# Attention on one core: the softmax sums' reciprocals are copied out of PSUM by ScalarE, earlier in a slot, and VectorE multiplies the context straight out of its PSUM bank, one step earlier

## The reference

```python
h = layernorm(x, gamma1, beta1)
Q = (h @ Wq + bq).reshape(B, T, 16, 32).transpose(0, 2, 1, 3)      # K and V alike
scores = jnp.einsum('bhqd,bhkd->bhqk', Q, K) / np.sqrt(32)
scores = jnp.where(causal, scores, -jnp.inf)
attn = jax.nn.softmax(scores, axis=-1)
ctx = jnp.einsum('bhqk,bhkd->bhqd', attn, V)
ctx = ctx.transpose(0, 2, 1, 3).reshape(B, T, C)
x1 = x + ctx @ Wo + bo
...
x2 = x1 + gelu(layernorm(x1) @ W1 + b1) @ W2 + b2
x = x + gate * (x2 - x)
```

## Time and profile before

| | |
|---|---|
| three runs | 1737.58, 1741.61, 1746.10 us; median 1741.61 |
| the profiled execution | 1743.59 us, of which the span from first to last instruction is 1741.6 |
| PE busy | 1660.3 us, 95% of the span |
| DVE, ACT, POOL busy | 1174.9, 976.4, 439.6 us |
| mean granted TensorE clock | 0.982 of full speed |

### The profile page before, as it was taken

One profiled execution on the slowest core, in us unless ns is written; L12 is line 12 of the kernel. 1 busy time (PEld: TensorE's weight loads), 2 busy tenths in 40 slices (PEclk: granted clock), 3 DMA queues, 4 the chain that ended last, 5 costly groups with the idle time before them and its releaser, 6 DMA issues.

```text
span 1741.6 us, 27454 instructions
## 1 busy us (share of the span) xinstructions
PE 1660.3 (95%) x9416; PEld 1335.6 (77%) x9416; DVE 1174.9 (67%) x2759; ACT 976.4 (56%) x2257; POOL 439.6 (25%) x670
## 2 busy tenths in 40 slices
PE   5899998899999999999999889999999999999999
PEld 3678766667676777776777558888999999999998
DVE  6899875776776768686866736767565656565643
ACT  5788853777676767676767654635242424242422
POOL 6788620323131322323232112010101010101010
PEclk9999998899999999999999989999999999999999
DMA  7122234343444435343433534576646464646451
GB/s 285 73 87 84 82 118 115 96 99 88 117 101 102 116 84 130 87 122 88 103 86 86 179 113 158 207 267 250 252 160 254 167 245 166 245 170 242 170 194 67
DMA packets 61826, 254.81 MB, mean 146 GB/s; under 512 B 10580, under 2 KB 15956, under 8 KB 45944
## 3 DMA queue, kind: packets, MB, share of 16 engines
q1 hardware_dynamic: 61688, 253.06, 44.6%
HBM read 153.93 MB, written 48.23 MB: 116 GB/s over the span
## 4 chain that ended last, share of the span: by engine, by line
PE 79%; DVE 9%; ACT 4%; DMA 3%; issue 2%; SPq 2%; POOL 1%; DVEq 0%; POOLq 0%; ACTq 0%
PE psum L82 21%; PE psum L84 20%; PE psum L83 20%; PE psum L1634 4%; PE psum L1662 4%; PE psum L1615 3%; PE psum L1540 2%; DVE psum L1167 1%; SPq L922 1%; ACT psum L1410 1%; PE psum L1558 1%; ACT k_exps L1420 1%; DVE k_tokens L1218 1%; DMA k_stack<-k_samples 1%; PE psum L1566 1%
## 5 line engine op out<-in xcount | busy, mean ns | idle before, releaser
L1410 ACT ACTIVATE psum<-psum,b_mx 128x512 f32<-128x512 f32 (+3 forms) x512 | 258.4, 506 | 200.7 <-DVE b_mx L1167 198.8
L1167 DVE CUSTOM_DVE_ANT_0 psum<-psum,b_mask 128x512 f32<-128x512 f32 (+3 forms) x512 | 244.7, 505 | 151.4 <-PE psum L1615 149.6
L2477 ACT ACTIVATE k_act<-k_stack_f,k_smalls 128x512 f32<-128x512 f32 x112 | 81.0, 723 | 337.3 <-DVE k_stack_f L2265 337.3
L1420 ACT ACTIVATE k_exps<-psum 128x512 f32<-128x512 f32 (+1 forms) x384 | 203.0, 530 | 21.9 <-PE psum L1634 19.9
L2118 POOL TENSOR_SCALAR k_result<-k_result,k_pb 128x512 f32<-128x512 f32 x32 | 59.9, 1887 | 449.1 <-DVE k_result L2184 449.1
L1634 PE MATMUL psum<-k_stack 98*128 98x512 f32 (+3 forms) x512 | 157.8, 350 | 13.3 <-ACT k_exps L1420 13.2
L2244 DVE TENSOR_TENSOR k_act_lo<-k_act,k_act_hi 128x512 fp32r<-128x512 f32 x112 | 77.4, 691 | 130.4 <-ACT k_act_hi L2480 130.4
L1615 PE MATMUL psum<-k_stack 96*128 96x512 f32 (+3 forms) x512 | 150.5, 336 | 2.3 <-ACT psum L1410 2.3
L82 PE MATMUL psum<-k_act_hi,k_w_hi 128*128 128x512 f32 x384 | 151.0, 393 | 0.6 <-DVE k_act_lo L2244 0.6
L83 PE MATMUL psum<-k_act_lo,k_w_hi 128*128 128x512 f32 x384 | 150.6, 392 | 0.0
L84 PE MATMUL psum<-k_act_hi,k_w_lo 128*128 128x512 f32 x384 | 150.3, 391 | 0.0
(11 more groups left out here) (368 smaller groups left out, 4568.0 us busy)
## 6 DMA issues: line engine op xcount, KB each, us to landing
k_stack<-w_factors SPq DMA_DIRECT2D x35, 1792.0 KB, 7.8
k_stack<-k_samples SPq DMA_DIRECT2D x384, 128.0 KB, 2.4
k_weights<-w_factors SPq DMA_DIRECT2D x17, 1792.0 KB, 7.7
x<-k_tokens SPq DMA_DIRECT2D x10, 1024.0 KB, 3.9
k_tokens<-x SPq DMA_DIRECT2D x8, 1024.0 KB, 4.9
d<-k_result SPq DMA_DIRECT2D x32, 256.0 KB, 2.5
k_raw<-x SPq DMA_DIRECT2D x8, 1024.0 KB, 4.9
k_raw<-d SPq DMA_DIRECT2D x8, 1024.0 KB, 7.0
```

The source lines that it names most:

```text
L1167: last = dve.tensor_tensor_reduce(got, got, mask[:, S - width:S], -INV_SQRT_DH, -2.0 * MASKED, ALU.add, ALU.min, mx[n % 2][:, h, t:t + 1])
L1410: act.activation(sc(n, u)[:, at:at + width], sc(n, u)[:, at:at + width], ACT.Exp, bias=mx[n % 2][:, h, t:t + 1], scale=-1.0, accum_out=sum ...
L1420: act.activation(exps[n % 2][:, h, at:at + width], by_key(n, u)[:, 0:width], ACT.Exp, scale=INV_SQRT_DH).then_inc(k_act, 1)
L2477: act.activation(act_f[:], whole_tile, ACT.Gelu, bias=small(smalls, "b1", 2 * pair % M + second)).then_inc(pair_gelu, 1)
```

## The change

Four things change together:

1. ACT no longer copies the context. It copies the turned reciprocals out of their bank (`recs_out`, into the same SBUF tile), one step after PE turned them, and that frees the bank (`pj_act` instead of `pj_dve`).
2. PE turns the reciprocals in step 3 of slots with g = 0, 1 or 2, and in step 6 of those with g = 3 (`recs_step`); before it was step 7 in all. `bank_uses` lists `bc` earlier to match.
3. DVE multiplies bank 1 by the copied reciprocals, and this multiplication now counts up `ctx_out`, for which `maxima(n, 0)` on PE waits.
4. DVE does this in step 7, after `max_unit(n, 7)`; before, it multiplied in step 8, after `maxima_out(n, 0)`.

```diff
+def recs_step(n):
+    return 6 if n % G == 3 else 3
 def bank_uses(n):
-    bc = [("bc", *divmod(n - 2, G), "dve")] if 0 <= n - 2 < GROUPS else []
+    bc = [("bc", *divmod(n - 2, G), "act")] if 0 <= n - 2 < GROUPS else []
...
     if g == 0:
-        return qk + each("st", b + 1, range(J), "dve") + bc + v + after_back
+        return qk + bc + each("st", b + 1, range(J), "dve") + v + after_back
     if g == 1:
-        return qk + each("tin", b + 1, range(T), "act") + bc + v
+        return qk + bc + each("tin", b + 1, range(T), "act") + v
     if g == 2:
-        return qk + each("tb", b + 1, range(J), "act") + bc + each("wo", b - 1, range(J - 1), "dve")
+        return qk + bc + each("tb", b + 1, range(J), "act") + each("wo", b - 1, range(J - 1), "dve")
...
         def ctx_high(n):
-            wait_taken(pool, ("bc", *divmod(n, G)))
+            pool.wait_ge(ctx_out, n + 1)
...
         def over_sums(n):
-            name = ("bc", *divmod(n, G))
-            wait_full(dve, name)
-            dve.wait_ge(ctx_out, n + 1)
-            dve.tensor_tensor(ctx_at(n), ctx_at(n), pj(name), ALU.mult).then_inc(pj_dve, 1)
+            wait_taken(dve, ("bc", *divmod(n, G)))
+            wait_context(dve, n, CTX_ORDER[-1])
+            dve.tensor_tensor(ctx_at(n), ctx_bank, ctx_at(n), ALU.mult).then_inc(ctx_out, 1)
...
-            if u == 8 and 0 <= n - 2 < GROUPS:
+            if u == 7 and 0 <= n - 2 < GROUPS:
                 over_sums(n - 2)
...
-        def context_out(n):
-            wait_context(act, n, CTX_ORDER[-1])
+        def recs_out(n):
+
+            name = ("bc", *divmod(n, G))
+            wait_full(act, name)
             if n >= G + 1:
+                act.wait_ge(cl_set, n - G)
                 wait_full(act, ("wo", (n - G - 1) // G, J - 1))
-            act.activation(ctx_at(n), ctx_bank, ACT.Copy).then_inc(ctx_out, 1)
+            act.activation(ctx_at(n), pj(name), ACT.Copy).then_inc(pj_act, 1)
...
-            if u == 7 and 0 <= n - 2 < GROUPS:
-                context_out(n - 2)
+            if u == recs_step(n) + 1 and 0 <= n - 2 < GROUPS:
+                recs_out(n - 2)
...
-            if u == 7 and 0 <= n - 2 < GROUPS:
+            if u == recs_step(n) and 0 <= n - 2 < GROUPS:
                 recs_back(n - 2)
```

## The result

| | before | after |
|---|---|---|
| median, lowest and highest of 7 executions | 1743.01 us (1737.38 to 1748.95) | 1760.28 us (1752.02 to 1763.11) |
| the profiled execution, its span | 1743.59, 1741.6 us | 1762.73, 1760.7 us |
| mean granted clock in it | 0.982 | 0.977 |

The ratio is 1.0078, with a 95% interval of 1.0058 to 1.0099: slower by 10 to 17 us. The kernel is slower, as forecast, and its median lies in the range of 1752 to 1782 but 9 us under the 1769.5. By the ratio the change costs 13.6 us, half of the 27.9 that I summed up; the two medians are 17.3 apart, the upper end of that interval. So the sign was right and the sum was not.

The account below looks back on a forecast made before the run. PE was taken to bound the kernel, busy 95% of the span. Waits of 14.3 us plus clock drops of 13.6 made 27.9 us on the median of 1741.61, forecasting 1769.5 us, with an 8-in-10 range of 1752 to 1782.

Parts of the forecast that it names:

- The release behind DVE's queue: Maxima transpose on PE waits for DVE's multiplication: 1.20 us later with g = 0, 0.83 with g = 3; 14.3 us in all.
- Nothing gives these back: PE has work queued behind the maxima transpose without another repeating wait, so the 14.3 us of added waits stay.
- the first term: The added PE waits at the transpose of the maxima, 14.3 us over all slots.
- PE's idle time of 1.8: With g = 0 PE was to stand idle 1.8 us before the maxima transpose, from about 655.86 on.
- The clock: Longer PE waits bring drops to half clock, 1.7 us each; 8 of 15 possible were taken, 13.6 us.
- The rest costs nothing: ACT's moved copy, the reciprocals' bank in step 3, later statistics and maxima going out were to add no time.
- Waits alone: Rival: the waits at the maxima transpose grow by 14.3 us but the clock stays, giving 1756; chance 0.22.
- The wait goes away: Rival: without ACT's hop the maxima transpose never waits, winning 14.3 us, giving 1727; chance 0.05.
- The bank of q is late: Rival: PE's step 3 claim stalls in perhaps five slots, 3 us more, with all 15 drops 1784; chance 0.04.
- no change: Rival: shorter waits behind the maxima transpose take back the added ones; 1745 if three quarters were absorbed; chance 0.07.

Follow-up runs that it names:

- experiment 2: Against the changed kernel, DVE's multiplication moved from step 7 to step 6 for g = 0, 1 and 2: 1751.67 us, ratio 1.0023 to the kernel before.
- experiment 3: Against the changed kernel, DVE's multiplication moved a step later, to step 8, in all slots: 1800.26 us, ratio 1.0308 to the kernel before.
- Experiment 4: Against the changed kernel, step 8's score matmul issued 13 times instead of once in 7 slots with g = 0: 1749.72 us, ratio 1.0021 to the kernel before.
- experiment 1: The changed kernel run again with no edit: 1759.21 us, ratio 1.0070 to the kernel before.
- experiment 5: Against the changed kernel, PE's transposes of the reciprocals and ACT's copy put back in step 7 in all slots: 1767.48 us, ratio 1.0108 to the kernel before.

## Why the prediction was right and wrong

- **The release behind DVE's queue: right, in place and size.** For g = 0 L1656 was to start 1.20 us later in its slot; it starts 16.21 us into the slot for 14.97, 1.24 later. For g = 3 it was 0.83, and it is 17.16 for 16.43, 0.73; the 0.1 is the signal from ACT to DVE, which I had put at 0.14 and which shows as 0.03. For g = 1 I said 0.1 earlier, and it is 0.05. For g = 2 there is no wait, as said. The waits came to 30.2 us in 23 waits over the whole span (25.8 between 400 and 1100 us), for about 29 predicted. Experiments 2 and 3 move the multiplication alone and the wait at this place follows it both ways; but with g = 0 the time follows only in part, since other waits come in for it (experiment 2).
- **"Nothing gives these back": nearly.** The slot with g = 0 grows by 1.07, not 1.24: 0.17 is absorbed behind the wait. Slot 28 grows by 0.56 alone, since its steps differ. Slots with g = 3 grow by 0.73. Over slots 4 to 30 the first term comes to 6 x 1.07 + 0.56 = 7.0 with g = 0 and 3.6 with g = 3: 10.6 us. The forecast of 14.3 is for all slots; for these it makes 7 x 1.20 + 6 x 0.83 - 0.7 = 12.7. Of my eight slots with g = 3 five grew by 0.57 to 0.75; slot 27 has a fall of the clock in both kernels and is nearly as long as before, slot 3 grew by 0.2, and slot 31 is the last.
- **PE's idle time of 1.8: too short, it is 2.14.** I took from PE's arrival the 0.22 that it had waited at the reciprocals. But step 7 became 0.75 shorter (1.28 to 0.53), and step 6 0.13, while step 3 took up only 0.44 (1.85 to 2.29). What left step 7 is 0.38 of transposes and a wait of 0.38: L1672 started 0.44 us behind the matmul before it, and in the changed kernel the score in its place starts 0.06 behind. The row shows 0.22 of that wait, since the modelled end of the matmul before covers the rest.
- **The clock: right in kind, mis-sized.** Experiment 4 shows that it is a cost of its own. I took 8 falls of 1.7 us, 13.6. There are 7, less the one of before, at 1.43 by experiment 1; what g = 0 gained beyond the waits is 15.0 - 7.0 = 8.0 us in six falls, 1.3 each. The error is in two parts. A fall costs less than half of the 3.40 us at half clock. In slots 12 and 20 that is so because 0.6 us of it lies in the wait; behind the wait, at 1.43 for 1.7, why is open, for PE is recorded as busy all through that stretch with the fall and without it. And I spread the falls over g = 0 and g = 3 alike, while none of the waits of 1.36 with g = 3 is followed by one, but for that in slot 27; nearly each wait of 2.14 is.
- **"The rest costs nothing": wrong, it gains.** With g = 2 no wait was there to lengthen, and I set the slot at zero. It got 0.40 shorter, 3.4 us in all. What I left out is the order of the banks. Each use waits until the last but one was taken out, and with g = 2 in step 7 it is ACT that takes them out, by L1437 (L1442 after). Slot 18 before:

```profile
697.39 0.78 ACT L1437 ACTIVATE k_samples<-psum,k_smalls 128x512 f32<-128x512 f32 x1
...
697.64 0.63 PE L1672 MATMUL psum<-k_ident,k_early 128*128 128x128 f32 x4
698.31 0.48 PE L82 MATMUL psum<-k_ch,k_wo_hi 128*128 128x512 f32 x1
```

  And slot 18 after, where the four transposes stand in step 3 and `wo` (L82) comes right behind the scores of step 7:

```profile
705.94 0.60 PE L1680 MATMUL psum<-k_ident,k_early 128*128 128x128 f32 x4
706.29 0.48 PE L1642 MATMUL psum<-k_stack 98*128 98x512 f32 x1
...
712.42 0.79 ACT L1442 ACTIVATE k_samples<-psum,k_smalls 128x512 f32<-128x512 f32 x1
...
713.35 0.47 PE L82 MATMUL psum<-k_ch,k_wo_hi 128*128 128x512 f32 x1
```

  From the first transpose to the matmul behind them it is 0.67 us before and 0.35 after. The transposes themselves aren't slower: they start 0.14, 0.11 and 0.11 apart before, and 0.11 apart after. What is longer is the wait behind them, which the row doesn't mark because the modelled end of the last transpose covers most of it. Before, `wo` waited for the last of ACT's four copies: 697.39 + 0.78 = 698.17, and 0.14 for the signal gives its 698.31. After, with the transposes no longer between, its last but one is a copy earlier: 712.42 + 0.79 + 0.14 = 713.35, again its start. The same holds in all slots with g = 2 from 6 to 26, in both kernels. I had read 0.38 in slot 16, used 0.40 for every slot, and didn't look at what follows. By the lengths of the steps, step 7 with g = 2 gets 0.69 shorter, step 3 0.45 longer, step 9 0.13 and step 8 0.05 shorter, together about 0.4. The expectation of experiment 5 calls these transposes dearer; it is the same wait.
- **The sum by what was measured:** 10.6 of waits, 8.0 of clock, less 3.4: 15.2 us. These terms are taken from the same slots, so their agreement with the 15.1 there is no test. Independent of them are the interval of the ratio (10 to 17), in which the sum lies, and experiment 4, which gives 8.6 for the clock from the times alone. The prediction had 14.3 + 13.6 + 0.
- **The rivals.** "Waits alone" gave 14.3 us, and the ratio says 13.6; yet it is not what happened. Its number is met by luck, because the clock's 8.0 make up for waits mis-sized by 3.7 and a gain of 3.4 that was not counted. "The wait goes away" is refuted by every row. "The bank of q is late" was 1.7 us in three waits, and became real only when the turn was in step 3 with g = 3. Less of the time is absorbed than "no change" needed.

## What to carry to other kernels

A release that another engine waits for should hang on as few queued instructions as can be: taking a hop out (ACT's copy) is no gain where the new releaser stands behind more work. What is to be read in the trace is when each engine's queue gets to the release, not how long the hop is. The four kinds of slots want different schemes: the best kernel here uses the old one where PE comes early and the new one where it comes late. Where banks are handed round in an order, moving one use changes who waits for whom at the next: here that gave back 0.40 us in each slot with g = 2. And a wait that grows from 0.4 to 2.1 us on the engine that bounds the kernel can cost as much again in clock, so such idle time is to be costed for both.

## What the runs showed of the hardware

- The clock of TensorE fell to 0.50 for 3.4 us at 11 of the 12 PE waits of 2.14 us in two executions of the changed kernel, and in the rows shown of experiment 1 behind one and not behind another with the same busy time (1.26 and 1.25 us in 3.40). Of the waits of 1.36 to 1.39 us in these two and in experiment 5 it followed 3 of 32; in experiment 3 it followed 6 of 8 of 1.5 us and 8 of 12 of 2.5 us. So the length of the wait alone doesn't decide.
- Such a fall cost 1.43 us, in a stretch in which PE is recorded as busy throughout; 3.40 at half clock would be 1.7. Where it began 0.6 us before the wait ended it cost 1.15.
- Twelve matmuls that compute nothing new, put in front of a wait in each of 7 slots, made the kernel 8.6 us faster by the ratios. The wait's end stayed where it was.
- Four 128x128 transposes took 0.35 us from the first one's start to the next matmul's where that one had nothing to wait for. Where it waited for a copy by ACT it was 0.67, and the timeline marked nothing of the wait but 0.04 us of idle time, under what it prints.
